# A macaron block on one core: weights loaded from ScalarE's queue, a later wait for the constants, and value tiles cleared inside the first expert layer

## The reference

```python
x = L0_attn_x                                   # (16, 512, 128) f32
x = x + 0.5 * ffn(layernorm(x), Wr, We)         # 8 experts, top 2 of 8, capacity 193 per expert
x = x + attn(layernorm(x), Wq, bq, Wk, bk, Wv, bv, Wo, bo)   # 16 heads of 8, causal, ALiBi
x = x + 0.5 * ffn(layernorm(x), Wr, We)         # the same router and experts

# ffn, per sequence
logits = x @ Wr.T;  top_vals, top_idx = top_k(logits, 2);  w = softmax(top_vals)
pos    = tokens before this one that picked the same expert;  keep = pos < C
out    = sum over the two picks of w * keep * (x @ We[expert])
```

## Time and profile before

| | us |
|---|---|
| median of 3 runs | 827.36 |
| lowest, highest | 826.97, 830.26 |
| profiled execution | 833.3 |
| span of the profiled execution | 831.6 |
| PE busy | 784.7 (94% of the span) |
| DVE busy | 736.9 (89%) |
| ACT busy | 637.5 (77%) |
| POOL busy | 538.7 (65%) |

### The profile page before, as it was taken

The page is one execution under the profiler, slowest core; times in us unless marked ns, Lnnn a source line. Parts: engine busy times, 40 slices in busy tenths (PEclk is TensorE's granted clock), DMA queues, the critical chain, the costliest instruction groups (busy, mean ns, idle before and its releaser), DMA issues. The chain is left out here.

```text
span 831.6 us, 23358 instructions
## 1 busy us (share of the span) xinstructions
PE 784.7 (94%) x6498; PEld 385.9 (46%) x6498; DVE 736.9 (89%) x2527; ACT 637.5 (77%) x1545; POOL 538.7 (65%) x838
## 2 busy tenths in 40 slices
PE   3998999989999999999999999999999999999996
PEld 2544544444444454454454444445444354445443
DVE  4799999988999999999999999999999838999996
ACT  2677777716988888888888888888878856776774
POOL 3687888855567567567467467467553436888787
PEclk9999999967999999999999999999999989999999
DMA  6700000332333233233233233233230000010011
GB/s 162 142 0 0 2 20 14 108 128 89 106 116 109 88 117 108 83 115 114 77 115 114 77 116 113 84 111 118 97 106 26 3 1 15 26 38 25 25 38 40
DMA packets 54974, 62.07 MB, mean 75 GB/s; under 512 B 5696, under 2 KB 48576, under 8 KB 54784
## 3 DMA queue, kind: packets, MB, share of 16 engines
q1 hardware_dynamic: 54912, 61.33, 23.1%
HBM read 31.70 MB, written 29.36 MB: 73 GB/s over the span
## 5 line engine op out<-in xcount | busy, mean ns | idle before, releaser
L1206 DVE TENSOR_REDUCE att_neg_max<-bank 128x1 bf16<-128x512 f32 (+3 forms) x704 | 409.4, 637 | 37.8 <-PE bank L967 34.4
L1078 ACT ACTIVATE att_probs<-bank 128x512 f32<-128x512 f32 x640 | 346.6, 596 | 55.2 <-PE bank L987 52.7
L1166 POOL TENSOR_SCALAR_AFFINE_SELECT att_probs<-att_probs 128x512 f32<-128x512 f32 x256 | 159.4, 635 | 203.6 <-ACT att_probs L1078 203.4
L987 PE MATMUL bank<-att_q_st,att_k_st 53*128 53x512 bf16 (+3 forms) x1024 | 211.7, 304 | 1.3 <-ACT att_probs L1078 1.1
L371 ACT ACTIVATE moe_scaled<-bank,moe_gates 128x128 f32<-128x128 f32 x512 | 145.3, 369 | 64.3 <-DVE moe_gates L550 32.0
L964 PE MATMUL bank<-att_k_st,att_q_st 51*128 51x384 bf16 (+2 forms) x768 | 180.9, 282 | 5.5 <-DVE att_neg_max L1206 4.2
L1004 PE MATMUL bank<-att_probs,att_v 128*32 128x512 f32 (+3 forms) x2048 | 178.7, 444 | 0.9 <-POOL att_probs L1166 0.4
L558 DVE SCALAR_TENSOR_TENSOR x<-bank,moe_gates,x 128x128 f32 (+1 forms) x512 | 159.7, 339 | 14.4 <-PE bank L303 10.8
L967 PE MATMUL bank<-att_k_st,att_q_st 64*128 64x128 bf16 x1024 | 160.1, 222 | 0.0
L964 PEld LDWEIGHTS bank<-att_k_st,att_q_st 51*128 51x128 bf16 x768 | 71.2, 95 | 176.7 <-DVE att_neg_max L1206 126.8
L303 PE MATMUL bank<-moe_we,moe_hT 128*128 128x512 f32 x256 | 137.8, 620 | 0.8 <-DVE x L1241 0.8
(11 more groups left out here) (83 smaller groups left out, 862.4 us busy)
## 6 DMA issues: line engine op xcount, KB each, us to landing
qk_parts<-att_parts SPq DMA_DIRECT2D x32, 384.0 KB, 2.5
att_q_st<-qk_parts SPq DMA_DIRECT2D x64, 192.0 KB
att_k_st<-qk_parts SPq DMA_DIRECT2D x64, 192.0 KB
qk_parts<-att_parts SPq DMA_DIRECT2D x32, 256.0 KB, 2.1
x<-in_L_attn_x SPq DMA_DIRECT2D x16, 256.0 KB, 3.1
qk_parts<-att_parts SPq DMA_DIRECT2D x32, 128.0 KB, 1.7
out<-x SPq DMA_DIRECT2D x16, 256.0 KB, 2.3
moe_we<-in_L_ffn_We SPq DMA_DIRECT2D x1, 512.0 KB, 5.1
```

Of the source, the lines that this page charges most:

```text
L987: mm = nc.tensor.matmul(exp_ps[m % RING][:, c:c + S - j * P], k_st[par][low:low + FINE_ROW, r, j * P:(j + 1) * P], q_st[par][low:low + FIN ...
L1078: nc.scalar.activation(probs[g % 2][:, n, :], exp_ps[m % RING][:], ACT.Exp).then_inc(exp_done, 1)
L1166: nc.gpsimd.affine_select(out=view, in_=view, compare_op=ALU.is_ge, fill=0.0, base=0, pattern=[[0, 4], [1, P]], channel_multiplier=-1).the ...
L1206: nc.vector.tensor_reduce(neg_max[par][:, g // 2, g % 2, heads[0]:heads[0] + len(heads), i], max_ps[m % RING][:, 0:len(heads) * width].rea ...
```

## The change

Four things are changed. First, `moe_we`, `moe_wrT` and the bf16 constants are issued by ACT, before everything else in its stream, and in that order; SP keeps x and the f32 constants. Secondly, DVE's wait for the constants moves behind the first sequence's statistics and shift; POOL's wait stays where it was. Thirdly, `set_v` is split in two: tile 0 is set at (5, 2) and tile 1 at (6, 2), in POOL's stream before the sums of tile 2 of these steps. Fourthly, the waits for `v_set` move from the early pieces of step 5 to the first copies of values.

```diff
+    def load(self, eng, n):
+        dst, src = self.loads[n]
+        eng.dma_start(dst[:], src).then_inc(self.placed, DMA)
...
             load(0, 0)
-            for dst, c in consts.loads:
-                sp.dma_start(dst[:], c).then_inc(consts.placed, DMA)
+            consts.load(sp, 0)
             load(1, 1)
-            weights.load(sp)
...
         def begin():
-            dve.wait_ge(consts.placed, consts.N_PLACED)
             statistics(0, 0, 0)
             aggregate(0)
             add_eps(0)
             shift_mean(0)
+            dve.wait_ge(consts.placed, consts.N_PLACED)
...
-EARLY = {(5, 1): ["spread"], (5, 3): ["bias"], (6, 1): ["statistics0"], (6, 3): ["aggregate0"],
+EARLY = {(5, 1): ["spread"], (5, 2): ["set_v0"], (5, 3): ["bias"], (6, 1): ["statistics0"], (6, 2): ["set_v1"], (6, 3): ["aggregate0"],
...
-    def set_v(self, pool):
-
-        for i in range(2):
-            self.nc.gpsimd.memset(self.v[i][:], 0.0).then_inc(self.v_set, 1)
-        pool.wait_ge(self.v_set, 2)
-        for i in range(2):
-            for ab in range(2):
-                one = ab * VS + HD
-                self.nc.gpsimd.memset(self.v[i][:, :, :, ab, one:one + 1], 1.0).then_inc(self.v_set, 1)
+    def set_v(self, pool, i):
+
+        self.nc.gpsimd.memset(self.v[i][:], 0.0).then_inc(self.v_set, 1)
+        pool.wait_ge(self.v_set, 3 * i + 1)
+        for ab in range(2):
+            one = ab * VS + HD
+            self.nc.gpsimd.memset(self.v[i][:, :, :, ab, one:one + 1], 1.0).then_inc(self.v_set, 1)
...
-                    pe.wait_ge(ops.v_set, ops.N_V)
...
             if what == "project_v":
+                if isinstance(b, int) and b <= 0:
+                    act.wait_ge(ops.v_set, ops.N_V)
...
-                    act.wait_ge(ops.v_set, ops.N_V)
...
+                elif what[:-1] == "set_v":
+                    ops.set_v(pool, int(what[-1]))
...
-                    dve.wait_ge(ops.v_set, ops.N_V)
...
         @block.scalar
         def _(act):
+            weights.load(act)
+            consts.load(act, 1)
             moe1.scalar.begin()
...
             moe1.gpsimd.begin()
-            ops.set_v(pool)
```

## The result

The changed kernel takes 831.25 us (median of 20 runs, 829.03 to 836.02), the kernel before 828.49 us (20 runs on the same chips). The ratio is 1.0033, 95% interval 1.0017 to 1.0049, that is +2.8 us (+1.4 to +4.1). The profiled execution is 830.0 us with a span of 828.3, so it is by itself shorter than the one before (833.3): two single executions don't show the change. The stages do.

A forecast was written before the change was run, and what follows sets the result against it. DVE was taken to bound steps 5 and 6, a single chain the start. Terms of 0.5 (start), 1.5 (step 5) and 1.7 (step 6) gave +3.7 us on 827.36, so 831.1 us, range 825.8 to 833.0.

The forecast's parts named there:

- What bounds: Steps 5 and 6: DVE almost without idle time sets the pace, PE waits for it, POOL has room.
- The start: Loads and first statistics: POOL's root waits for the bf16 constants, landing at 8.0 us instead of 5.76; +0.5 us.
- The hold: Steps 5 and 6: each late memset on POOL holds DVE's TENSOR_SCALAR L533 until the memset ends.
- The rival in which DVE goes first: Steps 5 and 6: L533 beats the memset both times; +1.2 us in all, 828.6 us, chance 0.15.
- The term of step 5: set_v0 in step 5 delays DVE, so out_bias and PE come 1.0 to 1.6 us later; taken as 1.5.
- The second hold: Step 5: L423, now at about 75.2 to 75.95, meets DVE's L539 and adds up to 0.6 us.
- the first hold: Step 5: the memset holds DVE's L533 until 74.9, making DVE 1.0 us later.
- The term of step 6: set_v1 in step 6 holds L533 and perhaps L539, reaching PE nearly whole; 1.2 to 2.1 us, taken as 1.7.
- The sum: Whole kernel: 0.5 + 1.5 + 1.7 = +3.7 us, giving 831.1 us for the median.
- The clock: Start of attention: low-clock stretch 8 us longer or shorter moves the time 4 us either way, 835 or 827; chance 0.08.

The follow-up runs named there:

- e6: Kernel before with one semaphore per table of constants, plus DVE's bias addition one tile earlier, at (5, 2): 827.13 against 829.32 us, ratio 0.9976.
- e1: Changed kernel with the memsets back at the start of POOL's stream, loads and waits as changed: 828.59 against 828.50 us, ratio 1.0006.
- e4: Changed kernel with the denominator computed by a SCALAR_TENSOR_TENSOR with two SBUF inputs, not a TENSOR_SCALAR: 830.38 against 829.32 us, ratio 1.0018.
- d3: Changed kernel with value tiles cleared at the start and one memset of twice the size at (5, 2): 833.2 against 829.32 us, ratio 1.0067.
- f1: Changed kernel with six additional matmuls on PE at the head of step 6, before its wait for out_bias: 836.49 us, ratio 1.0093.

## Why the prediction was right

The forecast was +3.7 us, and +2.8 (1.4 to 4.1) was measured. The mechanism held at each of the places that were named; the two holds were put too high. That the level came out so close (831.1 forecast, 831.25 measured) is luck: the kernel before was put at 827.36 by its first three runs and has 828.49 in twenty, and these 1.1 us too little cancel the 0.9 us too much of the difference. Point by point:

- *What bounds.* DVE sets the pace of steps 5 to 8: shown, by e6 above all.
- *The start.* The constants landed at 7.7 against a forecast of 8.0, and the root started at 7.76, with the wait moved from DVE to POOL. The term of +0.5 us is +0.27 between the first two profiles and 0.3 to 1.1 over all of them (the copy of the logits at 13.5 to 14.2 with the old loads, 14.5 to 14.6 with the changed ones). e1, which keeps this part alone, gives +0.5 us with an interval around zero. What the forecast didn't name is that the loads that stayed on SP came later too: the f32 constants took 5.0 instead of 2.5 us, though issued at 1.32 as before. It cost nothing, since the bf16 constants landed later still.
- *The hold.* L533, now L535, is held 1.69 us in both steps, and POOL comes first both times; e4 and d3 show that the kind of DVE instruction and the size of the memset decide. The rival in which DVE goes first did not occur, but its terms can be read off e4: -0.53 us in step 5 (forecast -0.5) and +0.83 in step 7 (forecast 1.2). So of the +1.33 in step 7 only 0.5 us go with the hold itself; the other 0.83 are POOL's own lateness at the root of sequence 9.
- *The term of step 5 was too large*: 1.5 us against 0.81, and PE's wait for `out_bias` grew to 2.97 us, not to about 3.7. Two things fell out of it. The second hold, of L539 by L423, did not come about, since L541 got in at 73.67, 0.01 us ahead of L425. And of the forecast 1.0 us of the first hold, 0.2 us came back because what stood behind L535 ended with it at 73.51 and not one after the other.
- *The term of step 6* was +1.7 us, measured +1.33 in the period of step 7, for the same reasons.
- *The sum.* The terms measured sum to 0.3 to 1.1 + 0.81 + 1.33 = 2.4 to 3.2 us, which is the whole of the measured +2.8.
- *The clock* was given a chance at the start of attention. There the stretch at the lower level did last 20.5 to 30.7 us by execution, in both kernels, and this moves single executions by some 2 us; the terms above give the measured difference without it. Not foreseen was that the clock can fall in step 6, behind an idle time of PE that the change itself lengthened from 2.17 to 2.97 us. It cost 1.3 us in the one execution of the changed kernel that shows it. How often it happens isn't known, and the interval of the total is too wide to show it.

## What to carry to other kernels

A wait that is moved to another engine is not removed: ask what the next instruction on the chain still waits for, and give each load its own semaphore. Work that is free in an idle stretch is not free in a full one, even on an engine with room: here a 1.80 us memset on POOL held DVE, which was full, for its whole length, and POOL's root behind it was late. Look for a TENSOR_SCALAR on DVE that starts within the span of such a memset, and write it with two SBUF inputs if it can't be moved (0.15 instead of 1.69 us). And a long wait on PE is worth nothing by itself if another engine's stream is full throughout.

## What was not expected of the hardware

- The granted clock fell to 0.5, in some executions only, after PE had idled 2.97 us or more between busy stretches (3 of 5 profiles), and in none of the 9 profiles in which this idle time was 2.2 us or less, f1 among them, where it was filled. It came up to 1.3 us after PE was back at work. That the idle time is the cause was not shown.
- The moment in the first 30 us when PE's matmuls halve their duration varies between executions of one kernel: step 0 took 12.39 and 9.59 us in the kernel before, 10.28, 12.43 and 10.21 in the changed one. That alone spreads single runs by almost 3 us. The clock in the profile does not tell: it reads 1.00 from 18 to 26 us as well, where two matmuls of 128x512 take about 2 us in the kernel before, against 1.02 us behind it.
- Twelve more matmuls on PE in the first layer came with a hole of 3.1 us in attention, 170 us later; its cause is open.
- The DMA issue of the bf16 constants, ACT's third, held its queue for 1.68 us, where the same issue on SP took 0.43 us. This is not peculiar to ACT: SP's own seventh issue (a load of x at 4.48) took 1.87 us in the kernel before. The cause is open.
